# A ranking network on one core: six groups of rows in the last but one tile, and a layer moved ahead of its products

## What is computed

```python
x0 = emb[ids].reshape(ids.shape[0], -1)
x = x0
for i in range(3):
    s = x @ cross_w[i]
    x = x0 * s[:, None] + cross_b[i] + x
h = relu(x0 @ w1 + b1)          # 1664 -> 1024
h = relu(h @ w2 + b2)           # 1024 -> 512
h = relu(h @ w3 + b3)           # 512 -> 256
logit = concat([x, h], axis=1) @ out_w + out_b
y = sigmoid(logit)
```

## Time and profile before

| | us |
|---|---|
| median of three runs | 539.59 |
| lowest, highest run | 538.75, 539.72 |
| span of the profiled execution | 535.0 |
| PE busy with matmuls | 469.5 (88%) |
| POOL busy | 379.1 (71%) |
| DVE busy, ACT busy | 184.6, 104.9 |

### The profile page before, as it was taken

The page is one execution under the profiler, slowest core; times in us unless marked ns, Lnnn a source line. Parts: engine busy times, 40 slices in busy tenths (PEclk is TensorE's granted clock), DMA queues, the critical chain, the costliest instruction groups (busy, mean ns, idle before and its releaser), DMA issues.

```text
span 535.0 us, 11277 instructions
## 1 busy us (share of the span) xinstructions
PE 469.5 (88%) x2876; PEld 435.6 (81%) x2876; DVE 184.6 (35%) x383; ACT 104.9 (20%) x194; POOL 379.1 (71%) x407
## 2 busy tenths in 40 slices
PE   0088599999898999899898999989899898999997
PEld 0088389898888989798897989889798887989996
DVE  5464523314142322424232241423233142323325
ACT  6495501101011110111111020111011011101111
POOL 5777667577777777777777777777777777777720
PEclk9999999999999999999999999999999999999999
DMA  7992111011111111111111111111111111111100
GB/s 230 229 365 80 25 23 29 23 30 26 30 30 27 30 30 28 28 30 31 26 31 28 29 29 29 29 28 29 30 28 28 31 26 31 28 28 29 28 10 2
DMA packets 21730, 25.17 MB, mean 47 GB/s; under 512 B 11335, under 2 KB 12322, under 8 KB 21666
## 3 DMA queue, kind: packets, MB, share of 16 engines
q0 software_dynamic: 12800, 13.13, 11.9%
q1 hardware_dynamic: 6800, 11.01, 6.0%
q10 hardware_dynamic: 2066, 0.31, 0.3%
HBM read 24.41 MB, written 0.01 MB: 46 GB/s over the span
## 4 chain that ended last, share of the span: by engine, by line
PE 51%; ACTq 12%; POOL 10%; issue 9%; ACT 6%; DMA 6%; DVE 5%; POOLq 0%; DVEq 0%
PE l_bank L714 39%; ACTq L389 11%; POOL x_raw L341 10%; DMA x_raw<-in_L_rec_emb,idx 5%; PE x_bank L714 4%; PE x_bank L730 3%; PE h_bank L758 3%; ACT xT_hi L402 2%; ACT w_hi L359 2%; DVE x_raw L520 2%; ACTq L386 1%; DVE xT_lo L527 1%; PE l_bank L789 1%; ACT h_bank L369 1%; DVE h2T_lo L532 1%
## 5 line engine op out<-in xcount | busy, mean ns | idle before, releaser
L341 POOL DMA_INDIRECT x_raw<-in_L_rec_emb,idx x400 | 378.3, 946 | 132.1 <-issue 104.4
L714 PE MATMUL l_bank<-w_hi,xT_hi 128*128 128x342 f32 (+1 forms) x624 | 145.2, 333 | 8.0 <-DVE xT_lo L527 7.9
L714 PE MATMUL l_bank<-w_lo,xT_hi 128*128 128x342 f32 (+1 forms) x624 | 137.9, 321 | 0.0
L714 PE MATMUL l_bank<-w_hi,xT_lo 128*128 128x342 f32 (+1 forms) x624 | 137.9, 321 | 0.0
L714 PEld LDWEIGHTS l_bank<-w_hi,xT_hi 128*128 128x128 f32 x624 | 103.4, 190 | 12.8 <-DVE xT_lo L527 11.4
L714 PEld LDWEIGHTS l_bank<-w_lo,xT_hi 128*128 128x128 f32 x624 | 106.8, 190 | 0.0
L714 PEld LDWEIGHTS l_bank<-w_hi,xT_lo 128*128 128x128 f32 x624 | 106.5, 190 | 0.0
L527 DVE TENSOR_TENSOR xT_lo<-x_bank,xT_hi 128x512 fp32r<-128x512 f32 (+1 forms) x66 | 38.2, 578 | 164.5 <-ACT xT_hi L402 164.5
L402 ACT ACTIVATE xT_hi<-x_bank 128x512 fp32r<-128x512 f32 (+1 forms) x66 | 33.5, 507 | 262.7 <-PE x_bank L730 199.7
L730 PE MATMUL x_bank<-identity,x_raw 128*128 128x128 f32 x208 | 34.9, 280 | 44.1 <-DVE x_raw L520 27.1
L730 PEld LDWEIGHTS x_bank<-identity,x_raw 128*128 128x128 f32 x208 | 25.2, 142 | 53.1 <-issue 50.5
(11 more groups left out here) (90 smaller groups left out, 289.4 us busy)
## 6 DMA issues: line engine op xcount, KB each, us to landing
ids<-in_L_rec_emb SPq DMA_DIRECT2D x1152, 0.2 KB
ids<-in_L_rec_emb ACTq DMA_DIRECT2D x896, 0.2 KB
w_raw<-in_L_rec_w SPq DMA_DIRECT2D x18, 512.0 KB, 21.3
x_raw<-in_L_rec_emb,idx POOLq DMA_INDIRECT x400, 2.8
b_rows<-in_L_rec_b SPq DMA_DIRECT2D x1, 512.0 KB, 9.4
b_rows<-in_L_rec_b SPq DMA_DIRECT2D x1, 256.0 KB, 7.5
ids<-in_r_ids SPq DMA_DIRECT2D x1, 208.0 KB, 2.7
b_rows<-in_L_rec_b SPq DMA_DIRECT2D x1, 128.0 KB, 8.0
```

The costliest lines, as they stand in the source:

```text
L341: pool.indirect_dma_start(out=dst, out_offset=None, in_=emb, in_offset=rows).then_inc(landed, 16)
L714: done = pe.matmul(bank[:, 0:b - a], x[:, k, :], w[:, k, a:b], start=(k == 0 and n == 0), stop=(k == last_k and n == 2))
```

## The change

Tile 14 (`TILES - 2`) gets groups of its own, `LAST_BUT_ONE`: six of 4, 3, 2, 2, 1 and 1 chunks in the order of the columns. Counters that took four groups for every tile (`NG * t`) become `before(t)`, the number of groups in all tiles ahead of t; tile 14 gets landing semaphores of its own as the last tile has. Each of PE, DVE and ACT gets a `last_but_one` step.

On PE, layer 3 of tile 13 goes from the end of step 14 to right behind `begin`, as in `last_step`, and the transposition of group 2 waits for DVE to have taken it out. On DVE, `l3_out(13)` goes from the end of the step to ahead of make_whole of group 2. On ACT the order stays, and x_hi of groups 4 and 5 stand behind the last fetch, ahead of `h1_hi`.

```diff
     LAST_GROUPS = [[0, 1, 2, 3], [4, 5, 6], [7, 8], [12], [9, 10], [11]]
     assert sorted(sum(LAST_GROUPS, [])) == list(range(K1))
+    LAST_BUT_ONE = [[0, 1, 2, 3], [4, 5, 6], [7, 8], [9, 10], [11], [12]]
+    assert sorted(sum(LAST_BUT_ONE, [])) == list(range(K1))
     def groups(t):
-        return LAST_GROUPS if t == TILES - 1 else GROUPS
+        return LAST_GROUPS if t == TILES - 1 else LAST_BUT_ONE if t == TILES - 2 else GROUPS
+    def before(t):
+        return sum(len(groups(u)) for u in range(t))
...
-        gathered_last = [sem(f"gathered_last{g}") for g in range(len(LAST_GROUPS))]
+        gathered_late = {t: [sem(f"gathered{t}_{g}") for g in range(len(groups(t)))] for t in (TILES - 2, TILES - 1)}
...
-                        read = next(i for i, old in enumerate(GROUPS) if ks[-1] in old)
-                        pool.wait_ge(x_transposed, NG * (t - 2) + read + 1)
-                    landed = gathered_last[g] if t == TILES - 1 else gathered[t % 2][g]
+                        read = next(i for i, old in enumerate(groups(t - 2)) if ks[-1] in old)
+                        pool.wait_ge(x_transposed, before(t - 2) + read + 1)
+                    landed = gathered_late[t][g] if t in gathered_late else gathered[t % 2][g]
...
-                act.wait_ge(x_transposed, NG * t + g + 1)
+                act.wait_ge(x_transposed, before(t) + g + 1)
...
                 fetch(ACT_SHARES[5])
                 h1_hi(t)
+            def last_but_one(t):
+                fetch(ACT_SHARES[0])
+                x_hi(t, 0)
+                fetch(ACT_SHARES[1])
+                h2_hi(t - 1)
+                fetch(ACT_SHARES[2])
+                x_hi(t, 1)
+                fetch(ACT_SHARES[3])
+                x_hi(t, 2)
+                if t in SP_TILES:
+                    sp_place(t)
+                if t in ACT_TILES:
+                    act_place(t)
+                fetch(ACT_SHARES[4])
+                x_hi(t, 3)
+                fetch(ACT_SHARES[5])
+                for g in range(4, len(groups(t))):
+                    x_hi(t, g)
+                h1_hi(t)
             def last_step(t):
                 x_hi(t, 0)
                 h2_hi(t - 1)
...
-                if t == TILES - 1:
+                if t in gathered_late:
-                        dve.wait_ge(gathered_last[g], 16 * sum(of_pool(t, f) for f in range(a, a + n)))
+                        dve.wait_ge(gathered_late[t][g], 16 * sum(of_pool(t, f) for f in range(a, a + n)))
...
                 h1_lo(t)
                 l3_out(t - 1)
+            def last_but_one(t):
+                begin(t)
+                l3_out(t - 1)
+                for g in range(2, len(groups(t))):
+                    make_whole(t, g)
+                    x_lo(t, g)
+                l1_out(t)
+                dots_out(t)
+                h1_lo(t)
             def last_step(t):
                 begin(t)
                 l3_out(t - 1)
...
-                if NG * t + g >= 2:
-                    pe.wait_ge(xT_ready, NG * t + g - 1)
+                if before(t) + g >= 2:
+                    pe.wait_ge(xT_ready, before(t) + g - 1)
-                    pe.wait_ge(x_whole, NG * t + g)
+                    pe.wait_ge(x_whole, before(t) + g)
...
                     l1(t, g, slice(-ahead(t), None))
                 transpose_h1(t)
                 l3(t - 1)
+            def last_but_one(t):
+                begin(t)
+                l3(t - 1)
+                l1(t, 1, BODY)
+                pe.wait_ge(h3_ready, t)
+                transpose_x(t, 2)
+                l1(t, 1, LAST)
+                l1(t, 2, BODY)
+                transpose_x(t, 3)
+                l1(t, 2, LAST)
+                l1(t, 3, BODY)
+                transpose_x(t, 4)
+                l1(t, 3, LAST)
+                transpose_x(t, 5)
+                l1(t, 4)
+                l1(t, 5)
+                transpose_h1(t)
             def last_step(t):
                 begin(t)
```

More of the change, by code:

```diff
@@ L75, in dcn_ranker_kernel @@
     HB = N1 // P // 2
-    assert N1 % P == 0 and N2 == 4 * P and N3 <= 512 and NG % 2 == 0 and HB * P <= 512
+    assert N1 % P == 0 and N2 == 4 * P and N3 <= 512 and all(len(groups(u)) % 2 == 0 for u in range(TILES)) and HB * P <= 512
     PACED = K1 - 1 + K2 - 1
@@ L171, in dcn_ranker_kernel @@
         x_bank = [pb(f"x_bank{i}") for i in range(2)]
-        assert all(len(ks) * P <= 512 - E for t in (0, TILES - 1) for ks in groups(t)[1::2])
+        assert all(len(ks) * P <= 512 - E for t in (0, TILES - 2, TILES - 1) for ks in groups(t)[1::2])
         end_bank = x_bank[1][:, 512 - E:512]
@@ L309, in other_engines_turn @@
                 if f == 4:
-                    pool.wait_ge(x_transposed, NG * (t - 1) + 3)
+                    pool.wait_ge(x_transposed, before(t - 1) + 3)
                 if f == 14:
@@ L315, in other_engines_turn @@
                     pool.wait_ge(l3_done, t - 1)
-                    pool.wait_ge(x_transposed, NG * t + 1)
+                    pool.wait_ge(x_transposed, before(t) + 1)
                 if f == 22:
@@ L479, in _ @@
             act.wait_ge(sp_idx_ready, 1)
-            for t in range(1, TILES - 1):
+            for t in range(1, TILES - 2):
                 step(t)
+            last_but_one(TILES - 2)
             last_step(TILES - 1)
@@ L524, in x_lo @@
             def x_lo(t, g):
-                dve.wait_ge(xT_hi_ready, NG * t + g + 1)
+                dve.wait_ge(xT_hi_ready, before(t) + g + 1)
                 ks = groups(t)[g]
@@ L739, in l1 @@
                     pe.wait_ge(dots_ready, t)
-                pe.wait_ge(xT_ready, NG * t + g + 1)
+                pe.wait_ge(xT_ready, before(t) + g + 1)
                 for k in ks:
```

## The result

The changed kernel takes 543.88 us (median of four runs, 543.46 to 544.95) against 539.17 us for the kernel before (537.08 to 539.72) beside it: the ratio is 1.0107, with a 95% interval of 1.0083 to 1.0131, so it is slower by 4.5 to 7 us where 3.5 was forecast. Two later comparisons, on two chips, gave 1.0096 (1.0060 to 1.0132) and 1.0097 (1.0072 to 1.0121).

A forecast was written before the change was run, and what follows sets the result against it. PE's own order in tiles 14 and 15 sets the end. New waits 0.49, 1.87, 2.11, 1.04 against old 1.31 + 0.48 and pipeline tails (about 2.0) cross-check +3.51 us: 539.59 becomes 543.1, range 541.8 to 544.8.

The forecast's parts named there:

- The wait until 480.70: PE in tile 14 before the change: 1.31 us for the second half of the rows to be made whole; forecast gone.
- POOL's check at field 16 of tile 15: POOL's wait for tile 15's first transposition: due at 502.35, transposition at about 501.6, so it clears by some 0.7 us.
- the rival of the clock: New PE waits in tile 14 lower TensorE's clock: 43% of 4 us, 1.7 us more, 544.8 us; chance 0.08.
- 3 us of work each time: Argument against a clock fall: PE has 3 us of work between the new waits in tile 14.
- the likeliest case: The forecast itself: slower by 3.51 us, 543.1 us, with TensorE's clock fall counted as nothing; chance 0.80.
- The conversion of group 2: ACT's x_hi of two chunks in tile 14, right after the fetch of 16: 481.85 to 482.23, 0.38 us.
- the second fetch: ACT's first fetch of 12 DMAs, ahead of group 3's conversion: begins 0.58 us after the conversion before it, lasts 4.04.
- the third: ACT's last fetch of 12 DMAs, ahead of group 4 and 5's conversions: begins 0.69 us after the conversion before, lasts 4.04.
- The handover: From h1's transpositions to layer 2 of tile 14, no longer covered by layer 3: 2.10 us, a PE wait of 1.04.
- 4.6 us lie around the span: Profiled span 535.0 us against the median 539.59: about 4.6 us taken as lying outside the span and added.
- Fetches that don't hold ACT: Rival: conversions come right behind their transpositions in tile 14; without any wait on a fetch -0.96 us, 538.6 us; chance 0.05.
- taken up in tile 15: Rival: gathers set tile 15's pace, so PE's lateness only shortens a wait there; no change, 539.6 us; chance 0.07.

The follow-up runs named there:

- the filled kernel: Changed kernel plus 12 throwaway PE products ahead of chunk 9 and 14 ahead of group 5's transposition: 542.23 us, ratio 1.0077; again 543.43 us, 1.0106.

## Why the prediction was right and wrong

**Direction and mechanism: right.** The wait until 480.70 is filled, the new waits stand where they were put, and the fetches cause them: without them the loss is gone, and the same fetches are free in the kernel before. Forecast and measured waits ahead of chunk 7, chunk 9, the transposition of group 5 and layer 2: 0.49 and 0.43, 1.87 and 1.90, 2.11 and 2.18, 1.04 and 0.70 (the measured ones by the idle time in the rows, which leaves out the last product's tail). From layer 2 to the end nothing changed. One thing came out otherwise: POOL's check at field 16 of tile 15, which was to clear by 0.7 us, held POOL for 2.74 us instead of the usual 0.30, as its timeline after the change shows:

```profile
507.03 0.94 POOL L348 DMA_INDIRECT x_raw<-in_L_rec_emb,idx  x1 [2.74 <-PE l_bank L753]
```

It cost nothing. The last gather starts at 515.78, 9.6 us before its rows are made whole (6.1 us in the kernel before), and PE waits nowhere in tile 15, as before.

**Size: too small, and the step that failed is the rival of the clock, which the sum put at nothing.** The stretch grew by 5.34 us where 3.51 was summed; 0.49 and 1.01 of the difference are chunks 11 and 12 at the lower clock. That rival had nearly the right price (1.7 us against 1.50) and far too low a chance (0.08). The argument against it took the wait of 1.31 us, which left the clock alone, as evidence for waits of 2 us, and "3 us of work each time" between them as protection. The work was there (3.2 us from 490.83 on) and did not protect: PE was busy 2.10 and 2.04 us of 4, then the clock fell, and in all five profiles of kernels with both or the first of these waits (unfilled) the clock fell within tile 14. The low level belonged in the likeliest case: 543.1 + 1.7 = 544.8, which was the very end of the range, against 545.4 by the ratio (1.0107 on the 539.59 of before). This account holds for the profiled executions; that the medians owe the same 1.5 us to the clock is not shown, since the two ratios of the filled kernel are 1.0077 and 1.0106.

In the Trainium skill, "TensorE: Matmul & The Clock Gate", section "What's actually happening", the low level follows idleness. The trace agrees with that. The prediction looked for one long wait, while here two of 1.90 and 2.18 us with work between them came ahead of the fall.

**Smaller terms.** Chunk 9 came 13.19 us after chunk 3 instead of 12.93, and group 5's transposition 18.58 instead of 18.15: 0.43 us. The conversion of group 2 came 0.07 us later after chunk 3 (7.07 against 7.00), the second fetch began 0.75 us after the conversion before it (485.10 to 485.85; 0.58 was taken), the third 0.76 (490.32 to 491.08; 0.69) and lasted 4.14 instead of 4.04: 0.41 of it. The handover came 2.01 us after the transpositions began instead of 2.10. Together 3.51 + 0.43 + 1.50 - 0.09 = 5.35, against 5.34.

**The frame.** That 4.6 us lie around the span was wrong: it set the span of one execution against the median of others. It is 1.8 us, and the executions differ. That moved no term of the sum, but it hid how quick the profiled execution was.

**The other rivals.** "Fetches that don't hold ACT" was tried by taking the fetches away: 19.09 us of stretch is 0.67 us less than before, where 0.96 was forecast, and the time is the same as before (0.9997). The Trainium skill, "DMA: Bandwidth & Descriptors", section "Rules for kernel authors", advises to issue a DMA early and to wait for it late. The rows show what the issuing itself takes: ACT is held 0.334 to 0.345 us for each DMA (5.34 for 16, 4.14 for 12). Nothing was "taken up in tile 15".

## What to carry to other kernels

Before work is cut into smaller pieces to fill a wait, follow each new piece through every engine that it passes, in that engine's own order: a conversion that stands behind a batch of DMA issues is as late as that batch, however small it is. A step that fills a hole early may have been the cover of another one late (here 1.31 us won, 1.16 given back), so price both ends. And price new waits of PE with the products behind them at the lower clock.

## What was not expected of the hardware

TensorE's clock fell behind waits of some 2 us, and not behind each of them. In tile 14 it fell after one wait of 1.89 us (1.11 us busy of 3.00), after waits of 1.69 and 1.90, and after waits of 1.90 and 2.18, where it had stayed at 1.00 behind the first; it stayed at 1.00 behind the wait of 1.31 in the kernel before. It can strike where nobody looks for it: in the kernel with the whole change and no fetches, PE waited 1.91 us in an earlier tile, and the stretch behind it (PE's busy time first, the granted clock behind POOL) shows the fall:

```profile
290.00:296.00 6.00, 4.09 (x28) 3.84 (x27) 0.72 (x1) 0.50 (x2) 4.59 (x5) 1.00 0.16 31
296.00:300.00 4.00, 4.00 (x18) 4.00 (x17) 1.14 (x2) 0.24 (x2) 2.97 (x4) 0.57 0.14 26
```

That execution still starts chunk 3 of tile 14 early, at 475.10. The other falls ahead of tile 14 all lie in the first 72 us of the profiles. The five profiles with a fall from 44 to 48 us (granted clock 0.57 to 0.85) start chunk 3 of tile 14 at 476.67 to 478.04, the nine without one at 474.85 to 476.75, and the kernel before was profiled only without. Whether the one causes the other is not shown.
